# Two graph layers on one core: the 256-deep hidden product of a sample pair in seven block products instead of four

## The reference

```
# layer 0, S = adj * adj, for each sample
h   = relu(layernorm(x))
h1  = relu(S @ (h @ W1))          # W1: 256 x 512
h2  = relu(S @ (h1 @ W2))         # W2: 512 x 1024
x   = x + S @ (h2 @ W3)           # W3: 1024 x 256
# layer 1, U = eigenvectors of the normalised Laplacian of adj
h   = relu(layernorm(x))
x   = x + U @ (relu((U.T @ h) @ V1 + b1) @ V2 + b2)
```

## Time and profile before

| | us |
|---|---|
| median of 3 runs | 2261.66 (2261.61 to 2262.51) |
| the profiled execution's own time | 2262.78 |
| its span, first to last instruction | 2261.1 |

### The profile page before, as it was taken

The page is one execution under the profiler, slowest core; times in us unless marked ns, Lnnn a source line. Parts: engine busy times, 40 slices in busy tenths (PEclk is TensorE's granted clock), DMA queues, the critical chain, the costliest instruction groups (busy, mean ns, idle before and its releaser), DMA issues.

```text
span 2261.1 us, 47549 instructions
## 1 busy us (share of the span) xinstructions
PE 2238.3 (99%) x12586; PEld 1905.3 (84%) x12586; DVE 1932.7 (85%) x10818; ACT 1151.1 (51%) x2901; POOL 1159.6 (51%) x1889
## 2 busy tenths in 40 slices
PE   8999999999999999999999999999999999999999
PEld 5777888888888888888888888888888888889998
DVE  7999999999888888888777778989999997547776
ACT  5555555555555555555555544444444444344554
POOL 6455555545555555555555557544555554343332
PEclk9999999999999999999999999999999999999999
DMA  3000000000000000000000000000000001024443
GB/s 105 29 29 29 16 24 29 29 29 20 29 29 29 29 29 19 19 28 28 28 28 28 28 29 20 29 29 19 24 25 28 28 28 38 19 80 132 135 132 107
DMA packets 90031, 90.14 MB, mean 40 GB/s; under 512 B 5376, under 2 KB 89088, under 8 KB 89856
## 3 DMA queue, kind: packets, MB, share of 16 engines
q1 hardware_dynamic: 89856, 88.23, 12.2%
HBM read 54.66 MB, written 33.55 MB: 39 GB/s over the span
## 4 chain that ended last, share of the span: by engine, by line
PE 91%; DVE 7%; ACT 1%; issue 1%; POOL 0%; DVEq 0%; ACTq 0%; POOLq 0%
PE ps L1550 74%; PE ps L1740 10%; PE ps L1472 3%; PE ps L1750 1%; DVE A L961 1%; PE ps L1683 1%; DVE A L965 1%; ACT squares L709 1%; DVE prods L998 1%; DVE xrow_sb L970 1%; ACT root_s L711 0%; DVE ps L1013 0%; DVE sc L979 0%; DVE sc L982 0%; DVE qcol L984 0%
## 5 line engine op out<-in xcount | busy, mean ns | idle before, releaser
L501 POOL COPY Eb<-sc 128x1 f32<-128x1 f32 (+1 forms) x254 | 46.7, 184 | 451.6 <-DVE v L986 231.9
L1550 PE MATMUL ps<-agg2T,w 128*128 128x256 f32 x1024 | 239.2, 379 | 0.0
L1550 PE MATMUL ps<-hid2T,xin 128*128 128x256 f32 x1024 | 236.1, 379 | 0.7 <-ACT h2T L754 0.7
L1550 PE MATMUL ps<-weightT,hid 128*128 128x256 f32 x1024 | 236.7, 379 | 0.0
L1550 PE MATMUL ps<-w,aggT 128*128 128x512 f32 x512 | 231.7, 592 | 0.0
L1550 PEld LDWEIGHTS ps<-weightT,hid 128*128 128x128 f32 x1024 | 189.5, 191 | 36.7 <-issue 14.3
L1550 PEld LDWEIGHTS ps<-hid2T,xin 128*128 128x128 f32 x1024 | 189.0, 190 | 26.2 <-ACT h2T L754 1.1
L1550 PEld LDWEIGHTS ps<-agg2T,w 128*128 128x128 f32 x1024 | 188.5, 190 | 25.3
L754 ACT ACTIVATE hid2T<-ps 128x512 f32<-128x512 f32 x256 | 151.0, 590 | 94.9 <-PE ps L1550 92.9
L1166 DVE SCALAR_TENSOR_TENSOR ahead<-ps,ne,ahead 128x14 f32<-128x14 f32 (+1 forms) x1020 | 189.9, 228 | 0.0
L1163 DVE RECIPROCAL ps<-ahead 128x14 f32<-128x14 f32 (+1 forms) x1024 | 188.3, 230 | 0.1
(11 more groups left out here) (387 smaller groups left out, 6194.3 us busy)
## 6 DMA issues: line engine op xcount, KB each, us to landing
xl<-in_x_dram SPq DMA_DIRECT2D x64, 256.0 KB, 2.8
xr<-in_x_dram SPq DMA_DIRECT2D x64, 256.0 KB, 2.8
x_dram<-xr SPq DMA_DIRECT2D x64, 256.0 KB, 2.3
xin<-x_dram SPq DMA_DIRECT2D x64, 256.0 KB, 2.8
out_dram<-xin SPq DMA_DIRECT2D x64, 256.0 KB, 2.2
w<-in_L_gnn_W_dram SPq DMA_DIRECT2D x1, 2048.0 KB, 10.3
w<-in_L_gnn_W_dram SPq DMA_DIRECT2D x1, 1024.0 KB, 12.2
w<-in_L_gnn_W_dram SPq DMA_DIRECT2D x1, 512.0 KB, 5.2
```

The lines of the kernel that those rows point to most:

```text
L501: pool.tensor_copy(Eb[:, bass.ds(k, 1)], sc[:, 4:5])
L1550: ins = pe.matmul(dst, a, b, start=start, stop=stop, skip_group_check=plan_.units[i][0][0] in "PG")
```

## The change

- The hid stage of a pair is one product of 512 x 256 (two samples of 256 rows each) by 256 x 512. It is cut in two each way: sample 0 and sample 1 as row halves, the 128-feature blocks in depth, two blocks of 256 columns of W1. Seven block products H1, H5, H6, H2, H7, H3, H4 replace the four units. Each is two matmuls of 256 columns, and each has one 128x512 evacuation.
- H6, H7 and H4 add onto bank 0, H3 onto bank 1. `bank_of` names the bank of each unit and `emptied` the unit whose evacuation a unit waits for.
- GpSimd forms four sums of `aggT` for the next pair (`sum_of_nodes`, 128x256 each, into the buffer `h`), three sums of kept products (`add_hid`, 128x512 each), and once four sums of W1. ScalarE gets three relu passes more (`finish_hid`).
- agg2's units wait for those relu passes (`hid_fin`) or for H4's evacuation.
- A pair has 43 units instead of 40; the positions in `REFINE_AT`, `TURN_AT`, `VECTORS_AT`, `NORMS_AT`, `COUNTS_AT`, `REFLECTORS_AT` are other ones.

```diff
-        COUNTS_AT, REFLECTORS_AT = 34, 3
-        REFINE_AT, TURN_AT, VECTORS_AT = (24, 27, 34, 38, 41, 43, 46), 63, 65
-        NORMS_AT = 22
+        COUNTS_AT, REFLECTORS_AT = 39, 7
+        REFINE_AT, TURN_AT, VECTORS_AT = (38, 41, 48, 50, 53, 55, 59), 75, 77
+        NORMS_AT = 33
...
-            units = [("hid", j, q) for j in range(2) for q in range(NB)]
+            units = [(p, 0, 0) for p in ("H1", "H5", "H6", "H2", "H7", "H3", "H4")]
...
+        BANK_OF = {"H1": 0, "H5": 1, "H6": 0, "H2": 2, "H7": 0, "H3": 1, "H4": 0, "agg": 2, "res": 2}
+        BANK_OF.update({p + n: 0 if n in "1674" else 2 for p in "PG" for n in "1567324"})
+        def bank_of(unit):
+            stage, j, q = unit
+            return (3, 2, 0, 1)[2 * q + j] if stage == "agg2" else BANK_OF[stage] + j
+        def emptied(plan_, i):
+            units = FULL.units + plan_.units
+            return max(n for n in range(PERIOD + i) if bank_of(units[n]) == bank_of(units[PERIOD + i])) - PERIOD
...
+        HID_ADDS = (("C11", "H1", "H2"), ("C12", "H6", "H3"), ("C22", "H5", "H7"))
...
-        POOL_ORDER = [("turn", n) for n in range(1, 5)] + [("add", n) for n in range(len(ADDS))]
-        POOL_ORDER += [("left", n) for n in range(len(LEFTS))] + [("g3", n) for n in range(len(G3_ADDS))]
+        POOL_ORDER = [("hid", n) for n in range(3)] + [("turn", n) for n in range(1, 5)] + [("add", n) for n in range(len(ADDS))]
+        POOL_ORDER += [("left", n) for n in range(len(LEFTS))] + [("nodes", n) for n in range(1, 5)] + [("g3", n) for n in range(len(G3_ADDS))]
...
-                    wanted = int((start + 0.4) // tau) if kind == "fin" else int(max(start - 3.2, 0) // tau)
+                    wanted = int((start + 0.4) // tau) if kind in ("fin", "hidfin") else int(max(start - 3.2, 0) // tau)
...
+            def sum_of_nodes(pair, n):
+                a11, a12, a21, a22 = (aggT[:, j, f, :] for j in range(2) for f in range(2))
+                a, b, op = {1: (a21, a22, ALU.add), 2: (node_block(1), a11, ALU.subtract), 3: (a11, a21, ALU.subtract),
+                            4: (a12, node_block(2), ALU.subtract)}[n]
...
+                pool.tensor_tensor(node_block(n), a, b, op).then_inc(node_sum, 1)
+            def add_hid(pair, n):
+                name, other, block_ = HID_ADDS[n]
+                pool.wait_ge(evac, before(pair) + FULL.at[block_, 0, 0] + 3)
+                pool.tensor_tensor(hid_block(name), hid_kept(other), hid_block(name), ALU.add).then_inc(hid_added, 1)
...
                     if isinstance(t, int) and t == 0:
                         if s == 0:
+                            pool.wait_ge(evac, 4)
+                            for n in range(1, 5):
+                                sum_of_nodes(0, n)
                             pool.wait_ge(load_w, 16 * 6)
...
             def pair_sums(pair, more, plan_=FULL):
+                for n in range(3):
+                    add_hid(pair, n)
                 for n in range(1, 5):
                     sum_of_moving(pair, n)
...
+            def finish_hid(pair, n):
+                act.wait_ge(hid_added, len(HID_ADDS) * pair + n + 1)
+                block_ = hid_block(HID_ADDS[n][0])
+                act.activation(block_, block_, ACT.Relu).then_inc(hid_fin, 1)
+            HID_AFTER = {5: [0], 6: [1], 7: [2]}
...
-                if stage == "hid":
-                    return group(bank[:, :], [(aggT[:, j, f, P * q:P * q + P], w1[:, f, :]) for f in range(FB)])
+                if stage[0] == "H":
+                    left, right = {"H1": (aggT[:, 0, 0, :], w1_block(0, 0)), "H2": (aggT[:, 0, 1, :], w1_block(1, 0)),
+                                   "H3": (node_block(4), w1_block(1, 1)), "H4": (aggT[:, 1, 1, :], w1sum[:, 3, :]),
+                                   "H5": (node_block(1), w1sum[:, 0, :]), "H6": (node_block(2), w1sum[:, 1, :]),
+                                   "H7": (node_block(3), w1sum[:, 2, :])}[stage]
+                    return [(half[m], left[:, P * m:P * m + P], right, "P" + stage[1] not in ONTO and m == 0, True)
+                            for m in range(NB)]
...
-                if stage == "agg2":
-                    pe.wait_ge(evac, before(pair) + plan_.at["hid", j, NB - 1] + 3)
+                if stage in ("H5", "H6", "H7", "H3"):
+                    pe.wait_ge(node_sum, 4 * pair + 4 + {"H5": 1, "H6": 2, "H7": 3, "H3": 4}[stage])
+                if (stage, j, q) == ("agg2", 1, 0):
+                    pe.wait_ge(evac, before(pair) + plan_.at["H4", 0, 0] + 3)
+                elif stage == "agg2":
+                    pe.wait_ge(hid_fin, len(HID_ADDS) * pair + (1, 1, 2, 3)[2 * q + j])
```

More of the change, by code:

```diff
@@ L338, in needs @@
                 stage, j, q = FULL.units[n]
-                out = [("evac", n - 4)] if n >= 4 else []
-                out += [("evac", 2 * j + 1)] if stage == "agg2" else []
+                out = [("evac", emptied(FULL, n))] if emptied(FULL, n) >= 0 else []
+                if stage == "agg2":
+                    out += [("evac", at["H4", 0, 0]) if (j, q) == (1, 0) else ("hidfin", (0, 0, 1, 2)[2 * q + j])]
                 if q == 0 and j == 0:
@@ L349, in needs @@
                 return [("add", n)]
+            if kind == "hid":
+                return [("evac", at[HID_ADDS[n][2], 0, 0])]
+            if kind == "hidfin":
+                return [("hid", n)]
+            if kind == "nodes":
+                return [("evac", at["agg", 1, 0])]
             if kind == "turn":
@@ L672, in pair_sums @@
                         ln_scale(pair + 1, j)
-                for kind, n in POOL_ORDER[4:]:
-                    in_turn(pair, kind, n, plan_)
+                for kind, n in POOL_ORDER[7:]:
+                    if kind != "nodes" or more:
+                        in_turn(pair, kind, n, plan_)
             with pool.Fori(WITH_STEPS, PAIRS - 1) as t:
@@ L746, in evacuate @@
                 else:
-                    dst = {"agg": aggT[:, j, :, :], "hid": hid[:, j, q:q + 1, :], "agg2": agg2T[:, j, 2 * q % H1B:2 * q % H1B + 2, :],
+                    dst = {"agg": aggT[:, j, :, :], "agg2": agg2T[:, j, 2 * q % H1B:2 * q % H1B + 2, :],
                            "res": res[:, j, :, :]}[stage].rearrange("p a n -> p (a n)")
@@ L846, in pair_body @@
                         finish(pair, n)
+                    for n in HID_AFTER.get(i, []):
+                        finish_hid(pair, n)
                     if more and (stage, j) == ("P2", 1):
@@ L1483, in unit_matmuls @@
                 stage, j, q = plan_.units[i]
[L1484 removed]
+                bank = ring[bank_of(plan_.units[i])]
                 half = [bank[:, 0:N], bank[:, N:2 * N]]
@@ L1518, in unit_waits @@
                 stage, j, q = plan_.units[i]
-                pe.wait_ge(evac, before(pair) + i - 4 + 3)
-                if stage == "hid" and q == 0 and isinstance(pair, int) and pair == 0:
-                    pe.wait_ge(evac, 3 + j)
-                if stage == "agg2":
-                    pe.wait_ge(evac, before(pair) + plan_.at["hid", j, NB - 1] + 3)
+                if not (isinstance(pair, int) and pair == 0 and emptied(plan_, i) < 0):
+                    pe.wait_ge(evac, before(pair) + emptied(plan_, i) + 3)
+                if stage == "H1" and isinstance(pair, int) and pair == 0:
+                    pe.wait_ge(evac, 4)
+                if stage in ("H5", "H6", "H7", "H3"):
[4 more added lines that the diff above has]
+                    pe.wait_ge(hid_fin, len(HID_ADDS) * pair + (1, 1, 2, 3)[2 * q + j])
                 if stage == "agg":
@@ L1549, in work @@
                 for dst, a, b, start, stop in mms[first:last]:
-                    ins = pe.matmul(dst, a, b, start=start, stop=stop, skip_group_check=plan_.units[i][0][0] in "PG")
+                    ins = pe.matmul(dst, a, b, start=start, stop=stop, skip_group_check=plan_.units[i][0][0] in "HPG")
                 if last == len(mms):
```

55 lines of the change are left out of this document (44 added, 11 removed).

## The result

The changed kernel takes 2305.58 us (median of 4 runs, 2303.87 to 2306.71) against 2261.89 (4 runs, 2261.61 to 2262.51): ratio 1.0192, 95% interval 1.0174 to 1.021. It is 1.9% slower. The profiled execution took 2305.52 us with a span of 2303.8, which is 42.7 more than the span before (2261.1). The forecast was 2297.0.

What follows compares the result with a forecast made beforehand. TensorE's full queue was taken to bound pairs 5 to 31, VectorE's chain pairs 0 to 4. Terms -22.3 + 28.4 + 7.6 + 2 + 6.6 + 11.0 + 2 + 0 = +35.3 us gave 2297.0 us, range 2268 to 2314.

Steps and rivals of the forecast that it cites:

- Matmuls: Hid stage on TensorE: 0.82 us less a pair, -22.3 us over pairs 5 to 31, 0 in the first five.
- Bank 0: H6, H7 and H4 wait for bank 0's evacuation, 0.09 us each time; more in slot 0: +7.6 us.
- First wait and root: agg2's first unit waits for evacuation, GpSimd sum and relu pass, +28.4 us; step 2's root late in pairs 11 to 20, +2.
- Pair 0: GpSimd's aggT sums ahead of the W2 and hid sums delay H5 and agg2: +6.6 us.
- pair 22: GpSimd's queued eigenvalue work makes agg2 12.0 us late, +11.0 us net; slow TensorE after the stop, +2.
- The end: Pairs 30 and 31, refinement and corrections: no sign which effect is larger, 0, bounds -1.5 and +3 us.
- A: Rival: waits are hidden, every pair gives 0.82 us, only pairs 22 and 0 cost: 2250 us, chance 0.12.
- B: Rival: quicker restarts, VectorE slack absorbs waits in pairs 5 to 10, first five pairs gain 0.82: 2273 us, chance 0.2.
- C: Rival: q's delay upsets later slots, steps 2 and 3 of 21 pairs, 1 us each: 2318 us, chance 0.13.

Runs made afterwards that it cites:

- e7: e3 with the seven products in four banks by turns, each started from zero, without accumulation in PSUM: 2243.57 us.
- e3: Changed kernel without the three sums of hid and their relu passes; agg2's units wait only for evacuations of their blocks: 2253.43 us.
- e4: Changed kernel with GpSimd's order altered in pair 0 (aggT and hid sums earlier) and pair 31 (layernorm scalars behind the hid sums): 2296.80 us.
- e6: Changed kernel with e2's order, C12's sum in slot 0, e4's ends and e1's cleared queue, but constants spread over pair 8: 2252.54 us.
- e2: Changed kernel with the products in the order H1, H2, H6, H5, H7, H3, H4, so block C11 is complete two products earlier: 2291.25 us.
- e1: Changed kernel with GpSimd's queue ahead of pair 22 cleared: constants at program start, crossed products and building of T later: 2291.96 us.
- e8: e6 with only the first two products ahead of q in slot 0 of the first five pairs: 2255.07 us.

## Why the prediction was right, and where it was off

The experiments split the 42.7 us by the prediction's own terms. Matmuls: e7 against before. Bank 0: e3 against e7. First wait and root: changed kernel against e3. Pair 0, pair 22 and the start: changed kernel against before. The end: changed kernel against e3. Each row is rounded.

```
term                                    predicted   measured
matmuls removed, pairs 5 to 31            -22.3       -22.4
the same, pairs 1 to 4                      0          -0.9
first wait of agg2, root behind it        +30.4       +30.3
bank 0                                     +7.6       +10.9
pair 0                                     +6.6        +6.1
pair 22, stop and slow clock              +13.0       +13.5
the end (pair 31)                           0          +4.9
before the first agg unit                   -          +0.4
sum                                       +35.3       +42.7
```

**Matmuls.** Right: columns count, and -0.82 a pair is there as soon as nothing waits (56.54 against 57.36). Pair 22 is the exception: it gives nothing even there (62.37 against 62.36), since GpSimd's queue sets when P5 starts. The prediction's sum had counted 0.82 for it. That fewer matmuls bring nothing in pairs 0 to 4 was nearly right, 0.9 of at most 4.1.

**First wait of agg2.** Right in mechanism; that the sum fits to 0.1 is luck of signs. The changed kernel against e3: pairs 1 to 4 6.3 (predicted 6.6), pairs 5 to 10 8.4 (7.4), pairs 11 to 20 11.0 (9.7 and 2 for the root), pair 21 0.7 (0.6), pairs 23 to 30 3.9, seven of them at 0.5 to 0.6 (predicted 0.51 each). Of the 0.52 us in a pair without steps, 0.41 stand at the first unit and the rest inside agg2.

**Bank 0.** Right in mechanism, too small in size. Three waits cost 0.14 each on average, not 0.09: I had counted 0.95 us for a bank's turn against 0.86 for the product between, and it is 1.00 (0.86 + 0.14). In pairs 12 to 20, where I had 0.09 for the pair, it is 0.23, since more than H6 waits (pair 16 of e3: 0.16 at H6 and 0.05 at H7). This is the one term of the sum, beside the end, whose size was clearly off.

**Pair 0.** Right within 0.5, but with two errors that cancel. GpSimd was free at 21.37, so H5 started at 22.15, not at 23.0, and agg2 at 31.60, not at 32.5. Behind both stops TensorE ran slowly: 3.32 us for 8 matmuls (from 22.15 to the next row at 25.47) where 1.73 are needed, which I had counted nowhere. e4 shows that GpSimd's order is the whole cause: with it turned, nothing of the 6.1 stays.

**Pair 22.** The stop was foretold at 12.0 and is 12.29. For the clock I took 2 between 0 and 2.5; 9.49 us against 6.91 is 2.6. With the 0.82 that pair 22 did not give, the forecast for the whole pair was 12.2, and it is 13.5. Windows of the changed kernel (from and to, length, busy us and count of PE, PEld, DVE, ACT, POOL, then TensorE's granted clock, DMA share, GB/s) show it:
```profile
1416.00:1424.00 8.00, 0.00 (x0) 0.00 (x0) 7.93 (x51) 0.00 (x0) 7.84 (x9) 0.66 0.00 0
1424.00:1426.00 2.00, 0.00 (x0) 0.00 (x0) 2.00 (x16) 0.00 (x0) 2.00 (x2) 0.50 0.02 4
1430.00:1432.00 2.00, 2.00 (x6) 1.55 (x6) 2.00 (x15) 1.12 (x2) 0.00 (x0) 0.50 0.00 0
1432.00:1440.00 8.00, 8.00 (x39) 7.04 (x38) 8.00 (x51) 3.18 (x8) 3.76 (x3) 0.99 0.00 1
```
The granted clock fell to 0.50 (the level of 1.2 GHz) while TensorE stood still and GpSimd worked, and stayed there for the first matmuls behind the stop. The rule that the prediction weighed, from the Trainium skill, TensorE: Matmul & The Clock Gate, Part 1, is the one that these rows bear out.

**The end.** This is the step that failed. "Pairs 30 and 31 ... I see no sign which is larger: 0, bounds -1.5 and +3." I had looked at the corrections and at VectorE, and noted that in pair 31 a refinement product stands between H4 and agg2, which I took as cover. I did not read what stands ahead of the three sums in GpSimd's queue there: `ln2_scalars(0, s)`, which waits for VectorE. It is the same fault as in pair 22, in the one other place of the program where GpSimd has other work between two pairs. It made +4.9 (changed kernel against e3): 3.0 of a stop and 1.8 of slow matmuls behind it, outside my bound. e4 got 4.0 of them back by GpSimd's order alone. The forecast stayed inside its range because this miss and that of the bank waits (3.3) are small against it, not because the end was understood.

**The rivals.** A, that the waits are hidden, falls: 31 of the 32 pairs of the changed kernel stop ahead of agg2. B had quicker restarts, slack of VectorE in pairs 5 to 10 and 0.82 us from each of the first five pairs. But the bank's restart is slower than mine, pairs 5 to 10 lost 8.4 us, and pairs 1 to 4 gave 0.9 in all. C, delays in later slots of 1 us a pair, shows only as VectorE's 0.5 us for the root in slot 2, which the forecast had: pairs 12 to 20 lose 1.06 us each (changed kernel against e3), where my two terms make 1.17. e6 shows what A would have been: 9.5 us faster than before, with 10.9 for the bank waits that stay.

## What to carry to other kernels

A product saved by Strassen's scheme (seven for eight) pays in sums, and their price is not their duration but their place: each sum that the next stage's first unit needs is a chain through an evacuation, GpSimd's queue and ScalarE's queue, and what of its latency is not covered by products behind the block's last one stops TensorE (0.5 us a pair without steps here, none with four products behind, e2). So complete first the block that is wanted first, and before work goes to a half-idle engine, read what is queued ahead of it in each stretch of the program, the seams between loops above all: 13.5 and 4.9 us of this change lay in two such seams, and moving GpSimd's instructions alone took back all of the first (e1) and 4.0 of the second (e4). The Trainium skill, PSUM — Partial Sum Buffer, Engine vs sequencer instructions, calls the queues of ScalarE, VectorE and GpSimd strict FIFO; the rows of pair 22 and of pair 31 are that rule with a price.

## What the hardware showed that I had not expected

A bank is free again about 1.0 us after the last matmul into it, with an evacuation of 0.60. The Trainium skill, Perfetto Trace Analysis, Matmuls, says to rotate independent groups through the banks so that an evacuation overlaps the next group. The trace agrees, and adds a size: one product of 0.86 us between two uses is not enough (0.14 us lost each time on average), three products are (e7, none lost).

TensorE pays twice for some short stops as well. Windows of the changed kernel in pair 0, behind the stop of 2.40 us, and in pair 31, behind the one of 3.03 (columns as above):
```profile
22.00:24.00 2.00, 1.85 (x5) 1.54 (x6) 0.00 (x0) 0.00 (x0) 1.84 (x4) 0.61 0.01 4
24.00:25.50 1.50, 1.50 (x5) 1.14 (x5) 0.00 (x0) 0.60 (x1) 1.50 (x2) 0.50 0.00 0
...
1983.00:1986.00 3.00, 3.00 (x11) 2.45 (x10) 0.00 (x0) 1.11 (x2) 0.00 (x0) 0.65 0.00 0
```
The granted clock is at its lower level for a while after either, and the matmuls take twice as long until it is back. But the length of the stop alone does not decide it. Pair 31 of e6 and then of e8, two kernels with the same instructions there and the same stop:
```profile
1926.84 1.99 PE L1814 MATMUL ps<-below,Z 128*128 128x256 f32 x8 [2.25 <-DVE below L1471]
1928.67 1.89 PE L1814 MATMUL ps<-Z,below 128*128 128x256 f32 x8
```
```profile
1927.46 3.05 PE L1814 MATMUL ps<-below,Z 128*128 128x256 f32 x8 [2.24 <-DVE below L1471]
1930.31 2.56 PE L1814 MATMUL ps<-Z,below 128*128 128x256 f32 x8
```
Eight matmuls took 1.83 us in the one and 2.85 in the other. What sets the difference these runs do not settle. For an estimate it is enough that, of the stops shown, those of 2.24, 2.40 and 3.03 us cost another 1.7, 1.6 and 1.8 us behind them, and that of 2.25 us in e6 cost nothing.
